# A state-space scan on one Trainium2 core: one C product for two units, written a column to the left

## The reference

```python
proj = hidden_states @ W_in.T
u, gate = jnp.split(proj, 2, axis=-1)                 # 1024 channels each
u = silu(causal depthwise conv of 4 taps (u) + conv_b)
dt, Bm, Cm = jnp.split(u @ Wx.T, [32, 32 + 16], axis=-1)      # each then RMS-normalised
delta = softplus(dt @ Wdt.T + dt_bias)
def step(state, xs):                                  # state: 1024 channels x 16
    d_t, B_t, C_t, u_t = xs
    dA = jnp.exp(d_t[..., None] * A)
    state = dA * state + (d_t * u_t)[..., None] * B_t[:, None, :]
    y_t = jnp.einsum('bdn,bn->bd', state, C_t)
    return (state, y_t)
y = (scan over the 2048 tokens + u * D_param) * silu(gate)
return y @ W_out.T
```

## Time and profile before

| what | value |
|---|---|
| median of 3 runs | 2009.27 us (2001.04 to 2016.91) |
| the profiled execution | 2000.12 us |
| its span, first to last instruction | 1998.3 us |
| mean granted TensorE clock | 0.817 of full speed |
| busy: PE, DVE, ACT, POOL | 1637.6, 1421.0, 1083.4, 1044.0 us |
| of these, POOL's C products, 256 | 600.1 us |
| POOL's drives, 128 | 301.6 us |
| DVE's scans, 1024 | 683.6 us |

### The profile page before, as it was taken

The page is one execution under the profiler, slowest core; times in us unless marked ns, Lnnn a source line. Parts: engine busy times, 40 slices in busy tenths (PEclk is TensorE's granted clock), DMA queues, the critical chain, the costliest instruction groups (busy, mean ns, idle before and its releaser), DMA issues. The chain is left out here.

```text
span 1998.3 us, 24406 instructions
## 1 busy us (share of the span) xinstructions
PE 1637.6 (82%) x8256; PEld 874.4 (44%) x8256; DVE 1421.0 (71%) x2404; ACT 1083.4 (54%) x1989; POOL 1044.0 (52%) x590
## 2 busy tenths in 40 slices
PE   6889999999689984979598797887978969745758
PEld 2522322232264443756265474654746646412422
DVE  3258888886183121058998989999899999999523
ACT  2334666667521112366757667576684766844227
POOL 0000000001063024059999999998999999999413
PEclk8766999999875985969598796987968869656778
DMA  5311000000193447043453434434444344444022
GB/s 220 150 56 49 3 3 3 3 3 4 37 350 136 132 121 268 24 108 77 104 121 83 119 91 106 121 91 103 109 101 111 85 104 116 104 103 103 24 103 85
DMA packets 150747, 191.58 MB, mean 96 GB/s; under 512 B 17715, under 2 KB 122947, under 8 KB 148958
## 3 DMA queue, kind: packets, MB, share of 16 engines
q1 hardware_dynamic: 142508, 167.19, 30.9%
q0 software_dynamic: 4608, 16.80, 2.3%
q10 hardware_dynamic: 3508, 6.05, 0.8%
HBM read 141.81 MB, written 48.18 MB: 95 GB/s over the span
## 5 line engine op out<-in xcount | busy, mean ns | idle before, releaser
L1758 DVE TENSOR_TENSOR_SCAN ssm_scan<-ssm_psum,ssm_state,ssm_scan 128x256 f32<-128x256 f32 x1024 | 683.6, 730 | 35.7 <-ACT ssm_psum L1634 35.2
L1341 POOL TENSOR_TENSOR ssm_scan<-ssm_scan,ssm_bc 128x1024 f32<-128x1024 f32 x256 | 600.1, 2361 | 51.6 <-DVE ssm_state L1761 51.5
L1634 ACT ACTIVATE ssm_psum<-ssm_rep,ssm_a 128x256 f32<-128x256 f32 x1024 | 433.5, 468 | 182.9 <-DVE ssm_scan L1758 182.4
L1465 PE MATMUL ssm_psum<-ssm_scan,ssm_select 128*32 128x256 f32 x2048 | 205.6, 484 | 208.8 <-POOL ssm_scan L1341 208.8
L1326 POOL TENSOR_TENSOR ssm_scan<-ssm_rep,ssm_bc 128x1024 f32<-128x1024 f32 x128 | 301.6, 2357 | 39.9 <-PE ssm_psum L1465 30.1
L677 DVE TENSOR_REDUCE att_rowmax<-att_psum 128x1 f32<-128x512 f32 x448 | 277.9, 681 | 39.7 <-PE att_psum L558 39.6
L640 ACT ACTIVATE att_probs<-att_psum 128x1024 f32<-128x1024 f32 x256 | 248.4, 1021 | 106.0 <-PE att_psum L576 105.7
L1465 PEld LDWEIGHTS ssm_psum<-ssm_scan,ssm_select 128*32 128x32 f32 x2048 | 45.9, 120 | 326.8 <-POOL ssm_scan L1341 224.2
L529 POOL COPY att_v<-v_tokens 128x128 f32<-128x128 f32 x8 | 2.3, 291 | 329.6 <-ACT att_out L634 329.6
L558 PE MATMUL att_psum<-att_k,att_q 72*128 72x512 bf16 x448 | 159.7, 396 | 3.7 <-DVE att_rowmax L677 2.2
L1743 DVE TENSOR_TENSOR ssm_scan<-ssm_rep,ssm_psum 128x1024 f32<-128x1024 f32 x128 | 155.4, 1214 | 7.4 <-PE ssm_psum L1465 4.2
(11 more groups left out here) (230 smaller groups left out, 1960.4 us busy)
## 6 DMA issues: line engine op xcount, KB each, us to landing
ssm_rep<-drive_rows SPq DMA_DIRECT2D x256, 256.0 KB, 4.3
qkv_wmod<-in_wmod SPq DMA_DIRECT2D x8, 1536.0 KB, 12.0
moe_we<-in_we SPq DMA_DIRECT2D x8, 1024.0 KB, 15.3
ssm_bc<-bc_rows SPq DMA_DIRECT2D x32, 256.0 KB, 4.9
drive_rows<-ssm_delta SPq DMA_DIRECT2D x64, 128.0 KB, 1.7
drive_rows<-ssm_du SPq DMA_DIRECT2D x64, 128.0 KB, 1.8
sorted_rows<-moe_zeros SPq DMA_DIRECT2D x1, 5888.0 KB, 19.3
moe_sorted<-sorted_rows SPq DMA_DIRECT2D x23, 256.0 KB, 3.4
```

Of the source, the lines that this page charges most:

```text
L1341: nc.gpsimd.tensor_tensor(scan[:, Q % RING], scan[:, Q % RING], bc[:, c % 2, 1, gr, :].unsqueeze(1).to_broadcast([P, J, SW]), ALU.mult).th ...
L1465: last = nc.tensor.matmul(ps_y[t % 2][32 * j:32 * j + 32, :], select[:], scan[:, Q % RING, j, :], start=(gr == 0), stop=False)
L1634: nc.scalar.activation(ps_decay[n % HALF_BANKS][:, i], rep[:, s % 2, 0, j, :], ACT.Exp, scale=amat[:, t, gr, j:j + 1]).then_inc(decay_done, 1)
L1758: nc.vector.tensor_tensor_scan(scan[:, Q % RING, j, :], ps_decay[(2 * Q + j // 2) % HALF_BANKS][:, j % 2], scan[:, Q % RING, j, :], state[ ...
```

## The change

- Each row of `scan` gets one more column (257 instead of 256). `drive` is the view of columns 1 to 256, in which the drives are written and the scans run. `read` is the view of columns 0 to 255.
- The C product is issued once for a pair, at the odd unit: it reads `drive` of two slots (2048 values) and writes `read`, a column to the left. The last state of each scan, in the last column, so stays unharmed by the product.
- The product waits for the pair's scans (`scan_done`), not for its carry. The carry is one tensor_reduce of 128 x 8 for the pair. `carry_done` counts pairs.
- `read_done` rises by 2 at the product of a pair.
- GpSimd's drive for unit Q+3 is issued behind the product of units Q-1 and Q. Before the loop the drives of units 0 and 2 are made.
- A drive on GpSimd also waits for the carry of the pair whose slot it takes.

```diff
-        scan = sb("ssm_scan", [P, RING, J, SW])
+        scan = sb("ssm_scan", [P, RING, J, SW + 1])
+        drive, read = scan[:, :, :, 1:], scan[:, :, :, 0:SW]
...
                 if Q >= RING:
                     pool.wait_ge(sum_done, Q - RING + 1)
-                nc.gpsimd.tensor_tensor(scan[:, Q % RING], rep[:, s % 2, 1],
+                    pool.wait_ge(carry_done, (Q - RING) // 2 + 1)
+                nc.gpsimd.tensor_tensor(drive[:, Q % RING], rep[:, s % 2, 1],
                                         bc[:, c % 2, 0, gr, :].unsqueeze(1).to_broadcast([P, J, SW]), ALU.mult).then_inc(pool_input, 1)
...
-            for Q in range(2):
+            for Q in range(4):
                 if not ON_DVE[Q]:
                     spread(Q)
...
-                    if Q + 2 < SCH * UNITS and not ON_DVE[(q + 2) % UNITS]:
-                        spread(Q + 2)
-                    pool.wait_ge(carry_done, Q + 1)
-                    nc.gpsimd.tensor_tensor(scan[:, Q % RING], scan[:, Q % RING],
-                                            bc[:, c % 2, 1, gr, :].unsqueeze(1).to_broadcast([P, J, SW]), ALU.mult).then_inc(read_done, 1)
+                    if gr % 2:
+                        pool.wait_ge(scan_done, (Q + 1) * J)
+                        pair = slice((Q - 1) % RING, Q % RING + 1)
+                        nc.gpsimd.tensor_tensor(read[:, pair], drive[:, pair],
+                                                bc[:, c % 2, 1, gr - 1:gr + 1, :].unsqueeze(2).to_broadcast([P, 2, J, SW]), ALU.mult).then_inc(read_done, 2)
+                        if Q + 3 < SCH * UNITS:
+                            spread(Q + 3)
...
-                    last = nc.tensor.matmul(ps_y[t % 2][32 * j:32 * j + 32, :], select[:], scan[:, Q % RING, j, :],
+                    last = nc.tensor.matmul(ps_y[t % 2][32 * j:32 * j + 32, :], select[:], read[:, Q % RING, j, :],
...
                 if c >= 1:
-                    dve.wait_ge(carry_done, Q - UNITS + 1)
+                    dve.wait_ge(carry_done, (Q - UNITS) // 2 + 1)
...
-                dve.wait_ge(scan_done, (Q + 1) * J)
-                nc.vector.tensor_reduce(state[:, t, gr, :], scan[:, Q % RING, :, SW - 1:SW], AX.X, ALU.max).then_inc(carry_done, 1)
+                if gr % 2:
+                    dve.wait_ge(scan_done, (Q + 1) * J)
+                    pair = slice((Q - 1) % RING, Q % RING + 1)
+                    nc.vector.tensor_reduce(state[:, t, gr - 1:gr + 1, :], scan[:, pair, :, SW:], AX.X, ALU.max).then_inc(carry_done, 1)
```

More of the change, by code:

```diff
@@ L1742, in spread @@
                     dve.wait_ge(sum_done, Q - RING + 1)
-                nc.vector.tensor_tensor(scan[:, Q % RING], rep[:, s % 2, 1],
+                nc.vector.tensor_tensor(drive[:, Q % RING], rep[:, s % 2, 1],
                                         ps_b[:, gr // 2, :].unsqueeze(1).to_broadcast([P, J, SW]), ALU.mult).then_inc(dve_input, 1)
@@ L1757, in unit @@
                         dve.wait_ge(decay_done, Q * J + j + 2)
-                    nc.vector.tensor_tensor_scan(scan[:, Q % RING, j, :], ps_decay[(2 * Q + j // 2) % HALF_BANKS][:, j % 2], scan[:, Q % RING, j, :],
+                    nc.vector.tensor_tensor_scan(drive[:, Q % RING, j, :], ps_decay[(2 * Q + j // 2) % HALF_BANKS][:, j % 2], drive[:, Q % RING, j, :],
                                                  state[:, t, gr, j:j + 1], ALU.mult, ALU.add).then_inc(scan_done, 1)
-                dve.wait_ge(scan_done, (Q + 1) * J)
-                nc.vector.tensor_reduce(state[:, t, gr, :], scan[:, Q % RING, :, SW - 1:SW], AX.X, ALU.max).then_inc(carry_done, 1)
+                if gr % 2:
+                    dve.wait_ge(scan_done, (Q + 1) * J)
+                    pair = slice((Q - 1) % RING, Q % RING + 1)
+                    nc.vector.tensor_reduce(state[:, t, gr - 1:gr + 1, :], scan[:, pair, :, SW:], AX.X, ALU.max).then_inc(carry_done, 1)
             def gate_y(s):
```

## The result

| | before | after |
|---|---|---|
| median | 2011.28 us (4 runs) | 2158.22 us (4 runs, 2154.33 to 2166.48) |
| ratio | | 1.0761, 95% interval 1.0722 to 1.0801 |
| span of the profiled execution | 1998.3 us | 2159.4 us |
| first to last scan | 999.9 us | 1149.9 us |
| granted TensorE clock | 0.817 | 0.808 |

What follows compares the result with a forecast made beforehand. DVE and POOL nearly full, PE pacing part of each chunk. Six chunks of 141.4 (848), 138.5 and 140 make 1127, less 3: 1124 against 1000; 2000.1 + 124 + 2 = 2126, a little added: 2128 us, range 2085 to 2168.

Steps and rivals of the forecast that it cites:

- What bounds the kernel: Scan loop before the change: DVE busy 117 and POOL 116 of 127 us a chunk, no engine with over 10% slack.
- Part 1, the product: On POOL, one product of 2048 elements takes 4.53 us instead of some 4.67 for two; 20 us saved, 0 to 45.
- Part 1, the stall: POOL's drive behind the product waits for PE's sum, 0.05+0.84 us; POOL's loop becomes 8.08 us, 8.52 at low clock.
- Part 2: PE and ACT get work later; a chunk walked by the largest of three limits per pair comes to 141.4 us.
- Pairs 8 to 12, POOL's loop: In the chunk walk, these five pairs go at POOL's pace, fast then low clock: 42.3 us together.
- places 0, 4, 6, 10, 12, 14: Places in a chunk where PE's block before an even sum feeds later scans: the loop is about 8.96 us.
- rival C: PE idles in light pairs, so its low clock spreads and blocks of 16 slow: another 35 to 50 us, 2170; chance 0.12.
- Chunk 6: Second-to-last chunk of the scan loop: it prepares less, so takes 138.5 us instead of 141.4.
- Part 3: 128 carry reductions go from DVE: 0.22 us a pair, 28 us, all off the path; bounds 0 and 28.
- This limit lies just under POOL's: DVE's own spread, waiting for the odd sum, finishes its pair after 11.5 us against POOL's 11.6; adds nothing.
- Part 4: Shifted read costs nothing; rows of 257 might cost 9 us in all by the 16-byte line rule, left out of the sum.
- Rivals B and D: B: only POOL's loop counts, 2066 us, chance 0.12. D: POOL's wait is covered, faster or level, 1980 us, chance 0.04.

Runs made afterwards that it cites:

- e1: The changed kernel with six slots instead of four in the ring of scans, convolution matrices shared between tile halves to make room; 2131.56 us, ratio 1.0630.
- e3: The kernel before with the column alone: rows of 257, each unit's product written a column to the left, a carry per unit still; 1991.18 us, ratio 0.9942.
- e4: The kernel before with the column and the carry once per pair, products still one per unit; 1991.19 us, ratio 0.9928.
- e6: The changed kernel with six slots, shared convolution matrices, and PE's block of the odd unit in front of the even sum; 1984.17 us, ratio 0.9879.
- e7: e4 with one wait added on PE: the even sum waits for the odd unit's product too; 2077.48 us, ratio 1.0344.
- e8: The kernel before with rows of 257 values in scan, 256 used, everything in place as before; 1997.49 us in one run.
- e9: e4 with rows of 257 in rep (replicated delta and delta*u) as well; 1985.19 us, ratio 0.9906.
- e11: e6 with rows of 257 in rep as well; 1981.61 us, ratio 0.9905.
- e12: The whole computation with rows of 257 in scan and rep, pair carry, product per unit, six slots, odd block before even sum, against the kernel before; 1957.29 us.

## Why the prediction was right, and where it was not

It forecast 2128 us, in 2085 to 2168; 2158 was measured. Direction, place and mechanism (sums withheld until the pair's product ends) were right, the size was 30 us short, and one stretch of the walk stood on the wrong loop.

- **What bounds the kernel.** "No engine has slack of more than 10%" holds for DVE and POOL alone: in the earlier trace rows PE is busy 108 of the 127 us and ACT 85. The forecast doesn't hang on it.
- **Part 1, the product.** 4.53 us was 4.16, outside the bounds 4.34 to 4.72. The fixed part of 0.19 us was right; the slope was not the same with rows of 257. The change itself had altered the price, and no row of before could have shown it. POOL's busy time fell by 61 us, not by 16 to 20.
- **Part 1, the stall.** "It waits for PE's sum of Q-1": 125 waits, 190 us; "near 128 times and over 110 us" was forecast. From product end to drive it took 1.03 us (1377.62+4.16 to 1382.81) where 0.89 was forecast: 0.14 to the sum instead of 0.05, and 0.89 behind it instead of 0.84. At the low clock POOL stood 1.40 to 1.48 us idle there. That makes POOL's loop 4.16+1.44+2.31, with 0.69 every second time, an estimate of 8.25 us; its pairs in the last chunk lasted 7.95 and 8.54 in turn. The chunk took 133.6 (140 was forecast with 4.53).
- **Part 2, the step that failed in part: the walk of a chunk, above all "Pairs 8 to 12, POOL's loop".** From the starts of the even sums on PE, in chunks 1 to 5:

| pairs | forecast | measured | e1, no wait for a slot |
|---|---|---|---|
| 0 to 7 | 70.6 | 72.8 to 74.4 | 73.1 to 74.5 |
| 8 to 12 | 42.3 | 44.5 to 45.2 | 43.3 to 43.4 |
| 13 to 15 | 28.5 | 26.3 to 27.9 | 26.9 to 28.1 |

  Pairs 10 and 12 did go at POOL's pace (8.5 us, forecast 8.86). Pairs 9 and 11 took 9.3 to 9.6 and 9.9, not 8.0 and 8.17, and pair 5 took 10.7, not 9. They wait for scans, in e1 as well. The prediction looked at blocks in front of even sums ("places 0, 4, 6, 10, 12, 14") and left out those at odd places, which stand directly behind the even sum and so behind the whole product. The convolution's block at place 9 holds back ACT's silu with its two table loads and then the decays of unit 13; the small ones at 19 and 21 hold back DVE's normalisation and ACT's softplus, and with them the scans of pairs 10 and 12. The rows, in the same order:

```profile
1374.79 2.68 DVE L1762 TENSOR_TENSOR_SCAN ssm_scan<-ssm_psum,ssm_state,ssm_scan 128x256 f32<-128x256 f32 x4 [3.92 <-ACT ssm_psum L1638]
...
1409.07 0.47 DVE L1730 SCALAR_TENSOR_TENSOR ssm_normed<-ssm_proj,ssm_lnw,ssm_psum 64x256 f32<-64x256 f32 x1 [1.20 <-PE ssm_psum L1437]
...
1422.63 0.69 DVE L1736 TENSOR_TENSOR ssm_delta<-ssm_delta,ssm_psum 128x512 f32<-128x512 f32 x1 [2.35 <-ACT ssm_psum L1607]
...
1430.72 4.16 POOL L1343 TENSOR_TENSOR ssm_scan<-ssm_scan,ssm_bc 128x2048 f32<-128x2048 f32 x1 [1.92 <-DVE ssm_scan L1762]
```

- **The clock, rival C, was partly in.** In the same chunk PE ran idle before the sum of unit 2 and took the next block, at place 3, at the low level:

```profile
1333.00 1.08 PE L1469 MATMUL ssm_psum<-ssm_scan,ssm_select 128*32 128x256 f32 x8 [3.55 <-POOL ssm_scan L1343]
1334.02 6.27 PE L1418 MATMUL ssm_psum<-ssm_upre,ssm_conv 128*128 128x256 f32 x16
```

  That is 2.6 us more than the 3.72 of the earlier trace rows. It is not so in every chunk: the six blocks at place 3 took 4.7, 5.4, 6.3, 4.7, 6.2 and 6.3 us, 11 us over in all, and pair 1, in which they lie, took 10.3 to 10.6 us with the shorter ones and 11.8 to 11.9 with the longer (8.9 to 9.0 was forecast).
- **The sum.** Chunks 1 to 5 took 145.9 each by the carries' rows (141.4 forecast), chunk 6 149.6, the last 133.6 (140). Chunk 6 was forecast lighter, at 138.5; it has the same blocks of 16 matmuls in PE's queue, and its pairs 4 to 6 took 31.6 us where chunks 1 to 5 needed 28.3, with two more slow blocks of 16 (5.4 and 4.8 us). That the total is only 30 us off owes something to luck: the product was taken 0.37 us too long, which made the last chunk and the pairs at POOL's pace too long, and the walk of the other pairs too short.
- **Part 3.** "28 us, all of it off the path": e3 and e4 agree. "This limit lies just under POOL's": DVE's drive waited for the odd sum 34.9 us in all, against 4.2 before; it was not always under.
- **Part 4.** The shifted read cost nothing (2179 ns in place, 2176 shifted). The rule of the Trainium skill on lines of 16 bytes (SBUF — State Buffer, under Door 1) gave an estimate of 9 us lost; the rows show no loss but 0.18 us gained per product.
- **Rivals B and D** fell with the time. D's condition, that POOL find the sum done, was met in e1, and the time there was still 2131.56: it was not enough. Only with the blocks in front as well (e6) is the joint product's kernel at 0.9879.

## What to carry to other kernels

Joining two instructions saves their fixed part (0.19 us here) and delays the first result by the whole second half; before doing it, ask who is queued behind the first result on the engine that consumes it, also with work that doesn't need it. An in-order queue that waits early should have its independent work in front of the wait. When two loops have nearly the same length, test them together: here opening one gave 27 or 71 us, opening both 174. And look at what an added wait holds up on every engine: the one of e7 was meant for one loop and closed both.

## What the runs showed of the hardware

GpSimd's float32 product of two inputs took 2.36 us for 128 x 1024 when both inputs had rows of 1024 bytes, and 2.18 when the rows of one lay 1028 bytes apart (products in e3 and e8, drives in e9, e11 and e12; the drives of e3 and e8, with rep still at 1024, stayed at 2.35). For 2048 elements it was 4.16 us; the step from 1024 to 2048 is 1.94 ns an element, against the 2.12 of before. The Trainium skill (GPSIMD Engine Reference, Instruction dispatch) calls about 2.5 cycles an element the floor of a two-input operation, an estimate of 2.08 ns at its 1.2 GHz; the joint product lies below it, at 1.94 ns by the step and at 2.03 with its fixed part (4.16 us for 2048). Why the distance of the rows matters was not tried, nor whether it is the distance itself or the addresses that the rows get by it.
